# Second expert layer in matmul tiles of 64 rows by 32 columns

## What is computed

```python
xn = layernorm(x, gamma, beta)
logits = einsum('bnd,des->bnes', l2norm(xn) * scale, l2norm(mu))
dispatch = softmax(logits, axis=1)                 # over the tokens
combine = softmax(logits.reshape(B, N, E * S), -1) # over all slots
slot_in = einsum('bnd,bnes->besd', xn, dispatch)
h = gelu(einsum('besd,edh->besh', slot_in, w1) + b1, approximate=False)
slot_out = einsum('besh,ehd->besd', h, w2) + b2    # the second expert layer
out = x + einsum('besd,bnes->bnd', slot_out, combine)
```

## Time and profile before

| | us |
|---|---|
| median of 3 runs | 648.91 (646.21 to 649.61) |
| the profiled execution | 647.36 |
| its span | 645.6 |
| matrix engine (PE) busy | 523.9 (81%) |
| its weight loads (PEld) busy | 371.5 (58%) |
| VectorE (DVE) busy | 417.8 (65%) |
| ScalarE (ACT) busy | 344.5 (53%) |
| GpSimd (POOL) busy | 286.1 (44%) |

### The profile page before, as it was taken

One profiled execution on the slowest core, in us unless ns is written; L12 is line 12 of the kernel. 1 busy time (PEld: TensorE's weight loads), 2 busy tenths in 40 slices (PEclk: granted clock), 3 DMA queues, 4 the chain that ended last, 5 costly groups with the idle time before them and its releaser, 6 DMA issues. The chain is left out here.

```text
span 645.6 us, 19721 instructions
## 1 busy us (share of the span) xinstructions
PE 523.9 (81%) x7660; PEld 371.5 (58%) x7660; DVE 417.8 (65%) x1187; ACT 344.5 (53%) x487; POOL 286.1 (44%) x369
## 2 busy tenths in 40 slices
PE   4658847888648999999984089999999995799996
PEld 2536635555214666666653045555656553799995
DVE  5468835666687898989824566556575730477775
ACT  3425623555317788888971126565655645544440
POOL 3113222222774687778501865677868522200000
PEclk9969978999757999999998579999999998799999
DMA  5453115540000111111110000322222222255553
GB/s 174 94 180 111 67 60 150 146 127 26 1 1 21 37 34 31 34 38 38 28 48 2 0 34 36 101 86 69 86 69 89 74 91 69 87 153 158 150 155 104
DMA packets 60912, 49.30 MB, mean 76 GB/s; under 512 B 15648, under 2 KB 50592, under 8 KB 60832
## 3 DMA queue, kind: packets, MB, share of 16 engines
q1 hardware_dynamic: 60832, 48.20, 24.2%
HBM read 30.87 MB, written 17.04 MB: 74 GB/s over the span
## 5 line engine op out<-in xcount | busy, mean ns | idle before, releaser
L545 DVE TENSOR_REDUCE c_mx<-ps 128x16 f32<-128x1024 f32 x64 | 78.1, 1220 | 18.7 <-PE ps L695 18.7
L523 POOL TENSOR_TENSOR c_k_bd<-c_k,w_mask 128x512 bf16<-128x512 f32 x80 | 83.8, 1078 | 0.0
L616 ACT ACTIVATE c_work<-ps 128x2048 f32<-128x2048 f32 x32 | 59.9, 1872 | 31.5 <-PE ps L723 31.5
L1255 PE MATMUL ps<-w_w,h_bd 128*64 128x128 f32 x1024 | 71.3, 279 | 6.2 <-DVE o_slot_out L1207 6.2
L1255 PEld LDWEIGHTS ps<-w_w,h_bd 128*64 128x64 f32 x1024 | 63.0, 140 | 7.1 <-DVE o_slot_out L1207 7.1
L1199 ACT ACTIVATE h_bd<-hidden 32x512 f32 (+1 forms) x64 | 40.2, 628 | 41.2 <-PE ps L1255 40.6
L1026 ACT ACTIVATE e_slot_in<-ps 128x1024 f32<-128x1024 f32 x32 | 32.8, 1023 | 51.9 <-PE ps L1084 51.9
L1231 DVE TENSOR_TENSOR o_slot_out<-ps,w_b 128x512 f32<-128x512 f32 x64 | 44.0, 687 | 20.6 <-PE ps L1255 20.2
L969 DVE TENSOR_REDUCE e_cm<-ps 128x16 f32<-128x1024 f32 x16 | 19.6, 1225 | 49.6 <-PE ps L1094 49.6
L1084 PE MATMUL ps<-e_disp,e_xn 64*128 64x256 f32 x256 | 36.3, 401 | 9.5 <-ACT e_slot_in L1026 8.2
L1269 PE MATMUL ps<-o_slot_out,ctx_sb 128*64 128x129 f32 x512 | 42.0, 274 | 1.2 <-DMA ctx_sb<-combine_scratch 1.2
(11 more groups left out here) (155 smaller groups left out, 1198.9 us busy)
## 6 DMA issues: line engine op xcount, KB each, us to landing
x_all<-x_scratch SPq DMA_DIRECT2D x128, 64.0 KB, 2.3
combine_scratch<-e_comb SPq DMA_DIRECT2D x16, 512.0 KB, 2.7
ctx_sb<-combine_scratch SPq DMA_DIRECT2D x16, 512.0 KB, 3.3
x_sb<-in_x SPq DMA_DIRECT2D x16, 256.0 KB, 3.0
ctx_sb<-in_ctx SPq DMA_DIRECT2D x16, 256.0 KB, 3.0
x_scratch<-a_x SPq DMA_DIRECT2D x16, 256.0 KB, 2.0
e_rden<-dispatch_inverses SPq DMA_DIRECT2D x64, 64.0 KB, 2.0
out<-o_y SPq DMA_DIRECT2D x64, 64.0 KB, 2.1
```

Of the source, the lines that this page charges most:

```text
L523: ins = nc.gpsimd.tensor_tensor(k_bd[:, c.m2, s, :], k32[:, c.v, :], w["mask8"][:, s:s + 1].to_broadcast([P, TOK]), ALU.mult)
L545: nc.vector.reduce_max(mx[:, c.m2, :, p], ps[:, SCORE:SCORE + 2, :].rearrange("p a (h m) -> p (a h) m", m=N), AX_X).then_inc(mx_sb.sem, 1)
L616: nc.scalar.activation(prob[:, h, :], ps[:, 0:4, :].rearrange("p a b -> p (a b)"), ACT.Exp, scale=float(HD) ** -0.5).then_inc(p_sb.sem, 1)
L1255: ins = nc.tensor.matmul(ps[64 * (g % 2):64 * (g % 2) + 64, p, at:at + D], h_bd[:, c.m2, s % 2 * PC + s // 2, g].rearrange("p e k -> p (e ...
```

## The change

The second layer is computed per pair of experts: the stationary side has 64 rows (two experts' hidden values) and 32 columns (two experts' slots), and `h_bd` holds half as much. Each matmul writes 32 partitions; the first two groups of experts (a = 0) fill one bank and the last two (a = 1) another, four positions at a time, so that a layer half (u) of 32 matmuls fills two banks. In the upper experts (8 to 15) the two pairs of a group swap their places in the partitions (`place`), in `hidden`, b1 and w2 alike; so the two matmuls that write the same 32 partitions take their rows from different halves. b1 and w2 are loaded in two pieces per group for it. The sums go to memory in another order, in three DMAs, the second half's rows swapped, and the matmul with ones writes them in that order; the division on GpSimd indexes accordingly. In the second stage the layer and the combination alternate by halves instead of quarters, VectorE adds b2 bank by bank in the same size as before, and all steps are written out, without a loop. The rest of the diff replaces dynamic indices by fixed ones.

```diff
@@ -368,6 +368,11 @@
         w[name] = kit.sb("w_" + name, shape)
 
 
+def place(expert):
+
+    return expert % 4 ^ (2 if expert >= EXPERTS // 2 else 0)
+
...
@@ -382,8 +387,10 @@
               (raw["mu"][:], a["L0_ffn_mu"].rearrange("d e s -> d (e s)")),
               (w["w1"][:], a["L0_ffn_w1"].rearrange("e d h -> d e h"))]
     for g in range(4):
-        loads.append((w["b1"][:, g:g + 1], a["L0_ffn_b1"][4 * g:4 * g + 4, :].rearrange("c (h o) -> (c h) o", o=1)))
-        loads.append((w["w2"][:, g, :], a["L0_ffn_w2"][4 * g:4 * g + 4].rearrange("c h d -> (c h) d")))
+        for i in range(2):
+            x, at = 4 * g + 2 * i, slice(HID * place(4 * g + 2 * i), HID * (place(4 * g + 2 * i) + 2))
+            loads.append((w["b1"][at, g:g + 1], a["L0_ffn_b1"][x:x + 2, :].rearrange("c (h o) -> (c h) o", o=1)))
+            loads.append((w["w2"][at, g, :], a["L0_ffn_w2"][x:x + 2].rearrange("c h d -> (c h) d")))
...
-    sums_out, sums_in = kit.sig("e_sums_out", 16), kit.pairs("e_sums_in")
+    sums_out, sums_in = kit.sig("e_sums_out", 48), kit.pairs("e_sums_in")
...
             c = t.plus(0)
             if c:
                 sp.wait_ge(raw_sb.sem, raw_sb.at(c))
-                sp.dma_start(sums_dram[c.v].rearrange("e (r q) -> e r q", r=2), raw[0:P:HID, c.m4, :, 1, :]).then_inc(sums_out.sem, 16)
+                halves = sums_dram[c.v].rearrange("e (r h q) -> e r h q", r=2, h=2)
+                sp.dma_start(halves[:, :, 0, :], raw[0:P:HID, c.m4, :, 1, 0:P]).then_inc(sums_out.sem, 16)
+                sp.dma_start(halves[0:2, :, 1, :], raw[2 * HID:P:HID, c.m4, :, 1, P:2 * P]).then_inc(sums_out.sem, 16)
+                sp.dma_start(halves[2:4, :, 1, :], raw[0:2 * HID:HID, c.m4, :, 1, P:2 * P]).then_inc(sums_out.sem, 16)
                 sp.wait_ge(sums_out.sem, sums_out.at(c))
...
-                nc.gpsimd.tensor_tensor(scaled[:, c.m2].rearrange("p (b g) k -> p b (g k)", b=2), raw[:, c.m4, :, 0, :],
-                                        rden[:, c.m2].rearrange("p s (b g) k -> p b g s k", b=2), ALU.mult).then_inc(divided.sem, 1)
+                nc.gpsimd.tensor_tensor(scaled[:, c.m2].rearrange("p (b g) (r x) -> p b g r x", b=2, r=2),
+                                        raw[:, c.m4, :, 0, :].rearrange("p b (g r x) -> p b g r x", g=2, r=2),
+                                        rden[:, c.m2].rearrange("p s g k -> p (s g k)").rearrange("p (r b g x) -> p b g r x", r=2, b=2, g=2), ALU.mult).then_inc(divided.sem, 1)
...
-                        ins = nc.tensor.matmul(ps[HID * e:HID * (e + 1), 6 + g // 2, at:at + P].rearrange("p (r q k) -> p r q k", r=2, q=PC),
+                        ins = nc.tensor.matmul(ps[HID * place(x):HID * (place(x) + 1), 6 + g // 2, at:at + P].rearrange("p (r q k) -> p r q k", r=2, q=PC),
...
-                            ps[HID * e:HID * (e + 1), 6 + r, 2 * P:4 * P].rearrange("p (q g k) -> p q g k", q=PC, g=4), w["ones"][at, 0:HID],
+                            ps[HID * e:HID * (e + 1), 6 + r, 2 * P:4 * P].rearrange("p (g q k) -> p q g k", q=PC, g=4), w["ones"][at, 0:HID],
                             disp[at, c.m2].rearrange("p q (g e k) -> p q g e k", g=4, e=4)[:, :, :, e, :], start=True, stop=True)
...
-    s_ps, s_sb = kit.sig("o_s_ps", 4), kit.sig("o_s_sb", 4)
+    s_ps, s_sb = kit.sig("o_s_ps", 2), kit.sig("o_s_sb", 4)
...
-    first, last, lo, hi = -2, CHUNKS, 2, CHUNKS - 2
+    steps = [Chunk(None, t) for t in range(-2, CHUNKS)]
...
-        def step(t):
+        for t in steps:
...
-                        sp.dma_start(out_v[bass.ds(c.v, 1), u, a].rearrange("o n r d -> (o n) r d"),
-                                     y[N * a:N * (a + 1), c.m2, 2 * u:2 * u + 2, :]).then_inc(y_out.of(c), 16)
-        walk(sp, step, first, last, lo, hi)
+                        sp.dma_start(out_v[c.v, u, a], y[N * a:N * (a + 1), c.m2, 2 * u:2 * u + 2, :]).then_inc(y_out.of(c), 16)
...
-                        h_bd[at, c.m2, :, :, e, :].rearrange("p s g k -> p g s k"),
-                        hidden[at, :, bass.ts(c.v, SC * SLOTS)].rearrange("p g (s k) -> p g s k", s=SC), ACT.Gelu)
+                        h_bd[at, c.m2, :, :, e % 2, :].rearrange("p s g k -> p g s k"),
+                        hidden[at, :, c.v * SC * SLOTS:(c.v + 1) * SC * SLOTS].rearrange("p g (s k) -> p g s k", s=SC), ACT.Gelu)
                 ins.then_inc(act_sb.sem, 1)
-        walk(act, step, first, last, lo, hi)
...
+        def shift(c, u, a):
+            if not c:
+                return
+            dve.wait_ge(s_ps.sem, s_ps.at(c, u + 1))
+            if c.plus(-2): dve.wait_ge(y_ps.sem, y_ps.at(c.plus(-2)))
+            nc.vector.tensor_tensor(slot_out[:, c.m2, 4 * u:4 * u + 4, a, 0:D], ps[:, 2 * u + a, :].rearrange("p (s d) -> p s d", s=4),
+                                    w["b2"][:, a:a + 1, :].to_broadcast([P, 4, D]), ALU.add).then_inc(s_sb.sem, 1)
...
-        def step(t):
-            for p in range(PC):
-                c = t.plus(1)
-                if c:
-                    dve.wait_ge(s_ps.sem, s_ps.at(c, p + 1))
-                    if c.plus(-2): dve.wait_ge(y_ps.sem, y_ps.at(c.plus(-2)))
-                    nc.vector.tensor_tensor(slot_out[:, c.m2, 2 * p:2 * p + 2, :, 0:D],
-                                            ps[:, p, :].rearrange("p (s a d) -> p s a d", s=2, a=2),
-                                            w["b2"][:].rearrange("p (o a) d -> p o a d", o=1).to_broadcast([P, 2, 2, D]),
-                                            ALU.add).then_inc(s_sb.sem, 1)
-                if p % 2:
-                    finish(t.plus(0), p // 2)
-        walk(dve, step, first, last, lo, hi)
+        for t in steps:
+            shift(t.plus(1), 0, 0)
+            shift(t.plus(1), 0, 1)
+            finish(t.plus(0), 0)
+            shift(t.plus(1), 1, 0)
+            shift(t.plus(1), 1, 1)
+            finish(t.plus(0), 1)
 
...
-        def step(t):
-            for p in range(PC):
-                c = t.plus(1)
-                if c:
-                    if p == 0:
-                        pe.wait_ge(act_sb.sem, act_sb.at(c))
-                    if c.plus(-1): pe.wait_ge(s_sb.sem, s_sb.at(c.plus(-1), p + 1))
-                    for s in range(2 * p, 2 * p + 2):
-                        for g in range(4):
-                            at = (s % 2) * 2 * D + (g // 2) * D
-                            ins = nc.tensor.matmul(ps[64 * (g % 2):64 * (g % 2) + 64, p, at:at + D],
-                                                   h_bd[:, c.m2, s % 2 * PC + s // 2, g].rearrange("p e k -> p (e k)"), w["w2"][:, g, :],
-                                                   start=True, stop=True)
-                    ins.then_inc(s_ps.sem, 1)
-                c = t.plus(0)
-                if c:
-                    if p == 0:
-                        pe.wait_ge(comb_in.of(c), comb_in.at(c))
-                        pe.wait_ge(s_sb.sem, s_sb.at(c))
-                    if p % 2 == 0:
-                        if c.plus(-1): pe.wait_ge(y_sb.sem, y_sb.at(c.plus(-1), p // 2 + 1))
-                    for r in range(2):
-                        s = 2 * p + r
-                        for h in range(2):
-                            ins = nc.tensor.matmul(ps[N * r:N * (r + 1), 4 + p // 2, (p % 2) * (D + 1):(p % 2 + 1) * (D + 1)],
-                                                   comb[:, c.m2, h, s * N:(s + 1) * N], slot_out[:, c.m2, s, h, :],
-                                                   start=h == 0, stop=h == 1)
-                    ins.then_inc(y_ps.sem, 1)
-        walk(pe, step, first, last, lo, hi)
+        def layer(c, u):
+            if not c:
+                return
+            if u == 0:
+                pe.wait_ge(act_sb.sem, act_sb.at(c))
+            if c.plus(-1): pe.wait_ge(s_sb.sem, s_sb.at(c.plus(-1), 2 * u + 2))
+            for i in range(4):
+                for q in range(4):
+                    for a in range(2):
+                        g, rows = 2 * a + q // 2, 64 * (q % 2 ^ a)
+                        ins = nc.tensor.matmul(ps[32 * q:32 * (q + 1), 2 * u + a, i * D:(i + 1) * D],
+                                               h_bd[rows:rows + 64, c.m2, (i % 2) * PC + 2 * u + i // 2, g].rearrange("p e k -> p (e k)"),
+                                               w["w2"][rows:rows + 64, g, :], start=True, stop=True)
+            ins.then_inc(s_ps.sem, 1)
+
+        def combine(c, h):
+            if not c:
+                return
+            if h == 0:
+                pe.wait_ge(comb_in.of(c), comb_in.at(c))
+                pe.wait_ge(s_sb.sem, s_sb.at(c))
+            if c.plus(-1): pe.wait_ge(y_sb.sem, y_sb.at(c.plus(-1), h + 1))
+            for p in range(2 * h, 2 * h + 2):
+                for r in range(2):
+                    s = 2 * p + r
+                    for a in range(2):
+                        ins = nc.tensor.matmul(ps[N * r:N * (r + 1), 4 + h, (p % 2) * (D + 1):(p % 2 + 1) * (D + 1)],
```

(35 more changed lines are left out.)

1 line of the change is left out of this document (removed).

## The result

The changed kernel takes 654.88 us (median; 654.05 to 658.29) against 647.56 (645.84 to 649.61) for the kernel before on the same chip: ratio 1.0123, 95% interval 1.008 to 1.0166. I had said 640.0. The profiled execution took 658.29 us, 3.4 above its median, with a span of 656.5 against 645.6.

The account below looks back on a forecast made before the run. The matmul stream was taken to bound the second expert stage. Terms +3.8 - 1.75 + 2.0 - 12.8 + 0.5 + 0.2 = -8.05 us gave 639.3 or 640.9, stated as 640; range 635.5 to 648.

Parts of the forecast that it names:

- writing out the stage: Second expert stage: unrolling the loop removes register work, included in SP's 2.96 us for four output stores; no cost given.
- weight loads: List ahead of the first store: eight more DMAs at 0.47 us lengthen VectorE's stall by 3.8 us (0 to 7.5).
- Sums on their way: Sums stored by three DMAs: nothing lost inside the first stage, 2.0 us at its end (1.4 to 3).
- The cold clock: Start of the last stage: the engine idles before the load lands, the clock may fall; 0.5 us added (0 to 2).
- The clear: GpSimd's clear of h_bd ahead of the first expert stage halves from 3.50 us; gain 1.75 (0 to 1.8).
- Tiles: Second stage: eight tiles at a time, layer half 1.03 us, combination half 1.06; matrix engine needs 4.18 us a chunk.
- What is late next: Second stage: VectorE sets the pace, 4.4 us a chunk against 5.25; gain 12.8 us (10.4 to 14.3).
- The first: Rival, second stage: a bank takes one row half at a time, four tiles together, chunk 5.94 us, time 663; 8%.
- The second: Rival, second stage: weight loads add up by columns; time 661, or 649 at 20 ns each; 6%.
- The third: Rival, second stage: period near 4.8 us from a slow combination load, both engines waiting for each other; 646; 13%.
- The fourth: Rival, first stage: strided write or late sums use up VectorE's slack; up to 7 us more, 647; 5%.
- fifth: Rival, list ahead of the first store: the added loads cost nothing; 636; 6%.

Follow-up runs that it names:

- the late loads: Changed kernel with the 32 loads of b1, w2 and b2 issued behind the stores of chunks 8 to 15, not ahead of the first store: 639.17 us.

## Why the prediction was wrong, point by point

**The step that failed: writing out the stage.** The prediction gave the loop's end only a gain ("register work of the loop included, which goes when it is unrolled") and asked of the records only whether the array takes them at 13.6 ns, not where they come from. The written-out stage takes its program in while it runs, one 16 KB packet per 254 PE records, and the change raises the rate of records from 37 to 73 a microsecond. The two edits are each harmless: written out with the old tiles 78.71 us, new tiles in the loop 67.16. Together the stage took 80.99, 78.28 and 76.83 us in three kernels with this program (the third, the late loads), in the mean 78.7, what it was before, where the prediction had 15 × 4.4 = 66. That the stops hang on PE's own program and on the loads is shown by taking either away, and that they are its packets' by their places, 254 PE records or a multiple apart. That the packet waits behind the load's packets, and the engine for the packet, is the reading that fits the times; the profile names no waiter for it. Why the engine goes on only 2.3 to 2.9 us after the packet is open.

**The mis-sized term: weight loads.** +3.8 predicted, +6.3 measured. The step took 0.47 from a whole-width piece for one on 64 partitions, and left the eight old slots at their price. Its upper bound of 7.5 held it. The +6.3 is no accident of two profiles: VectorE goes on at 42.1 us in the mean of five kernels with the 16 narrow pieces and the rest of the list unchanged (41.53 to 42.81), at 35.8 in the mean of three with the old list (35.34 to 36.40).

**Sums on their way: right for the stores, but not all of what the stretch lost.** +2.0 predicted. Six kernels with the three stores and the new tiles have 26.28 to 28.31 us between the stages, mean 27.0; four with one store and the old tiles 24.23 to 24.87, mean 24.5. The stretch lost 2.5. Timeline of SP in the changed kernel, against 541.04 of the earlier trace rows:

```profile
547.06 0.56 SPq L901 DMA_DIRECT2D dispatch_sums<-e_raw  x1
547.66 0.50 SPq L902 DMA_DIRECT2D dispatch_sums<-e_raw  x1
548.20 0.48 SPq L903 DMA_DIRECT2D dispatch_sums<-e_raw  x1
549.75 0.34 SPq L906 DMA_DIRECT2D e_sums<-dispatch_sums  x1
```

From the first store to the load of the sums 2.69 us, 1.0 more than before (541.04 to 542.74), and the same again at 554.89. The rest isn't the stores'. With the three stores and the old tiles the stretch is 25.96 us, with one store and the new tiles (no swap) 25.42. What comes with the new tiles stands in SP's timeline: the last four loads of the inverses take it 2.15 to 2.94 us in the eight kernels with the new second layer (2.61 in the changed one), and 1.71 in the five with the old. Why is open. Inside the first stage nothing is lost: 143.04 us against 143.10, so the writes in runs of 16 cost nothing, as taken.

**The cold clock: too small in the changed kernel.** 0.5 was given; its first three halves lose 2.4 after a wait of 3.6 us for the load. In the loop version the wait is 1.3 us, and the granted clock is 1.00 from 565.25 to 568.50.

**The clear: right.** It takes 1.79 us instead of 3.50. From VectorE's resumption to the first w1 matmul five kernels with the small `h_bd` need 354.6 us in the mean (353.2 to 355.9), four with the large one 356.2 (355.4 to 357.9): −1.7, of the size of the scatter.

**Tiles: right. What is late next: the number right, the engine not, and in that there was luck.** A chunk takes 4.35 us where nothing stops, 4.48 in the mean of the loop version, against 4.4. But the 4.4 was VectorE's (4.30 and up), and the matrix engine was to need only 4.18. Its halves came out at 1.09 and 1.09 instead of 1.03 and 1.06: the excess that the prediction reads as the cost of a change of tile shape is some 0.2 us (1.09 against 0.87 for the layer, against 0.90 for the combination), not 0.16. So the matrix engine sets the pace of the changed kernel where nothing stops, and VectorE waits for it; in the loop version the two come out even (VectorE has one wait, of 0.2 us, from 596 to 626.5). Timeline of VectorE in the changed kernel, in a stretch without a stop:

```profile
591.23 1.29 DVE L1225 TENSOR_TENSOR o_slot_out<-ps,w_b 128x512 f32<-128x512 f32 x2 [0.18 <-PE ps L1268]
```

Of the gain of 12.8 us, 78.72 − 67.16 = 11.6 are there in the loop.

**The rivals.** The first (a bank takes one row half at a time) is refuted, and its price was good: 5.94 predicted for four tiles, 5.97 measured in the version without the swap. Its "fewer than 4.5 tiles" was wrong by its own terms: with the 4.75 us that the other terms cost, a chunk may take 4.93 us, a record 19.5 ns, and that is 109 / 19.5 = 5.6 tiles. By the wide sentence of the Trainium skill ("TensorEngine Tiling (Array Packing)", Gotcha 1) the time would have been 663 for that reason; the narrow one ("PSUM — Partial Sum Buffer", section on bank collisions), same bank and same quarter, agrees with the 1.09 us. The second (weight loads add up) is refuted by the same 1.09. The third, 4.8 a chunk, fell short of the 5.25 of the written-out stage (78.7 / 15) and named another cause. The fourth and fifth did not come. None named the supply of instructions, so "slower" had too little chance: the range was built from the costs of steps that I saw, and the one I didn't see was worth 11 us.

**Sum, with the measured terms:** +6.3 − 1.7 + 2.5 + 0 = +7.1, and the medians differ by 7.3. The 2.5 and the 0 are means over several versions, not terms of this one kernel; in its own profile, 3.4 us above its median, they are 2.9 and 2.3.

## What to carry to other kernels

When a change makes instructions smaller and more numerous, work out the engine's rate of instructions and look where its program comes from: try such a stretch in a loop, whose later rounds here needed no packet of program, above all beside large transfers. Price a DMA by a row of the same shape, and a piece by the slot of every piece it replaces, not only the added ones. And a list of loads ahead of the first store is a place to look first: moving it gave 8.5 us here without any new tile.

## What was not expected of the hardware

The written-out program costs one 16 KB packet on q8 per 254 PE records; in the loop none came between 593 and 631 us. At 54 records a microsecond, with 127 GB/s of data, it kept up; at 73 the engine stood 6.3 to 8.5 us in 77 to 81, and 1.3 when most of the data was left out. After the stop of 2.12 us matmuls ran at a granted clock of 0.56 for 3.6 us, and the stop of 1.85 us in the version with the loop but for PE was followed by a layer half of 1.89 us; after the one of 2.40 us the clock stayed at 1.00 (598.47, 1.09). And an issue on SP took 0.60 us for a piece on 64 partitions and 0.43 on 128, each alike for the small b1 and the large w2, but 0.46 for the b2 pieces on 16.
